# Node stage after the distance layer of a graph network: attention terms as 16 more columns of the table product, one row buffer for both tables, two PSUM banks per step

## The reference

```python
# layer 0, after its edges have been summed into agg
out = agg @ w2.T + b2
out = ssp(out) @ w3.T + b3
x = x + out                                   # written as x1
# layer 1, per node
h = jnp.maximum(_layernorm(x, axis=-1), 0.0)
hh = (h @ W0.T).reshape(n, 8, 32)             # written as tab1
a_s = jnp.sum(hh * att_src, axis=-1)          # 8 per node
a_d = jnp.sum(hh * att_dst, axis=-1)          # 8 per node
```

## Time and profile before

| what | us |
|---|---|
| median of 3 runs (lowest, highest) | 5398.98 (5395.08, 5399.30) |
| the profiled execution's own time | 5395.97 |
| span of that profile | 5394.1 |
| stage n1: its first transfer is issued at | 1451.24 |
| stage n1: its last table tile is written to SBUF by | 1667.7 |
| first transfer of the next stage is issued at | 1676.9 |
| PE busy in 1505 to 1621 (116 us) | 111.67 |
| DVE busy in the same stretch | 76.71 |
| ACT busy in the same stretch | 31.23 |

### The profile page before, as it was taken

One profiled execution on the slowest core, in us unless ns is written; L12 is line 12 of the kernel. 1 busy time (PEld: TensorE's weight loads), 2 busy tenths in 40 slices (PEclk: granted clock), 3 DMA queues, 4 the chain that ended last, 5 costly groups with the idle time before them and its releaser, 6 DMA issues. The chain is left out here.

```text
span 5394.1 us, 106431 instructions
## 1 busy us (share of the span) xinstructions
PE 4401.4 (82%) x24965; PEld 3546.0 (66%) x24965; DVE 3865.9 (72%) x8445; ACT 1994.5 (37%) x3783; POOL 3395.0 (63%) x3492
## 2 busy tenths in 40 slices
PE   5999999999895888888885655555556899999793
PEld 4888888888675888888884555555555566666431
DVE  5999999999764887888788544444446677877673
ACT  3666666666424655655554300000003000000370
POOL 2677777777414777777640477777773777777473
PEclk8999999999997988999897777777787999999796
DMA  6333333333234555555535333333335111111243
GB/s 199 115 105 103 103 104 103 104 105 102 79 117 110 135 127 126 129 125 129 123 84 158 111 110 109 109 109 109 107 104 162 39 40 40 38 35 29 61 114 109
DMA packets 452024, 555.48 MB, mean 103 GB/s; under 512 B 213168, under 2 KB 322148, under 8 KB 451552
## 3 DMA queue, kind: packets, MB, share of 16 engines
q0 software_dynamic: 154128, 374.88, 25.6%
q1 hardware_dynamic: 290585, 172.07, 11.8%
q10 hardware_dynamic: 6840, 3.36, 0.3%
HBM read 497.40 MB, written 59.40 MB: 103 GB/s over the span
## 5 line engine op out<-in xcount | busy, mean ns | idle before, releaser
L507 POOL DMA_INDIRECT l_rows<-tmp_tab,l_idx x832 | 882.2, 1060 | 376.2 <-issue 252.2
L1170 POOL DMA_INDIRECT l_rows<-tmp_tab,src_sb x832 | 791.8, 952 | 321.8 <-issue 236.1
L1890 POOL DMA_INDIRECT l_rows<-tmp_tab,src_sb x812 | 767.7, 945 | 253.0 <-issue 236.5
L1976 PE MATMUL l_psa<-l_sel,l_rows 128*128 128x128 f32 x3248 | 571.2, 348 | 413.2 <-issue 222.6
L1976 PEld LDWEIGHTS l_psa<-l_sel,l_rows 128*128 128x128 f32 x3248 | 529.9, 255 | 454.5 <-issue 256.2
L2128 POOL DMA_INDIRECT l_rows<-tmp_tab,src_sb x695 | 656.5, 945 | 235.5 <-issue 201.3
L805 PE MATMUL l_psw<-l_fw,l_ssp 128*128 128x256 f32 x3328 | 763.2, 382 | 0.0
L1916 DVE TENSOR_TENSOR acc<-acc,l_psa 128x256 f32 x832 | 350.9, 422 | 536.8 <-PE l_psa L1976 445.1
L805 PEld LDWEIGHTS l_psw<-l_fw,l_ssp 128*128 128x128 f32 x3328 | 616.0, 190 | 154.1 <-issue 77.3
L2239 PE MATMUL l_found<-l_tabs,l_hot 128*128 128x384 f32 (+1 forms) x1872 | 651.7, 502 | 0.0
L1490 PE MATMUL l_psa<-l_sel,l_rows 128*128 128x128 f32 x3328 | 597.7, 308 | 57.2 <-DVE acc L1390 55.4
(11 more groups left out here) (355 smaller groups left out, 7747.8 us busy)
## 6 DMA issues: line engine op xcount, KB each, us to landing
l_rows<-tmp_tab,src_sb POOLq DMA_INDIRECT x2339
l_edge<-in_edge_t SPq DMA_DIRECT2D x104, 256.0 KB
l_own<-tmp_tab SPq DMA_DIRECT2D x1280, 1.0 KB
l_own<-tmp_tab ACTq DMA_DIRECT2D x1280, 1.0 KB
l_own<-tmp_tab ACTq DMA_DIRECT2D x1280, 0.2 KB
l_own<-tmp_tab SPq DMA_DIRECT2D x1280, 0.2 KB
tmp_x<-n_X SPq DMA_DIRECT2D x39, 512.0 KB
n_X<-in_x SPq DMA_DIRECT2D x26, 512.0 KB
```

The source lines that it names most:

```text
L507: nc.gpsimd.indirect_dma_start(out=rows[r][:, t, :], out_offset=None, in_=table[:, :], in_offset=bass.IndirectOffsetOnAxis(ap=idx[q][:, j: ...
L1170: nc.gpsimd.indirect_dma_start(out=rows[r][:, j, :], out_offset=None, in_=dram["tab1"][:, :], in_offset=bass.IndirectOffsetOnAxis(ap=sh["s ...
L1890: nc.gpsimd.indirect_dma_start(out=rows[g % ROWS][:, t, :], out_offset=None, in_=table[:, :], in_offset=bass.IndirectOffsetOnAxis(ap=sh["s ...
L1976: last = nc.tensor.matmul(by_tile(g)[0:n, t, k * P:(k + 1) * P], left[:, f:f + n], sel[b][:, t, :], start=True, stop=True)
```

## The change

`nodes_schnet` is rewritten. What it computes and stores is the same.

- `watt` is copied behind the 256 columns of `gat_w_t` into one matrix `wt` of 272 columns, so a table tile is two products of 272 columns, and the 128x16 products go. The bias row `gb` gets 16 zeros.
- The 272 columns of a tile are written to `O` by one DVE addition; ACT's two copies and the buffer `A` go. Both stores on POOL read `O` (columns 0 to 263 for `tab1`, 256 to 271 for `att_tab`).
- PSUM: `psZ` for `hidden`, `psY` for `output`, `psT` for the transposes, `psW` for the tables, two banks each and one copy of each. `hidden` waits for the softplus of the chunk ahead, `output` for the addition of the one ahead. The tables go tile by tile through the two banks of `psW`: tile t waits until tile t-2 has been added into `O`.
- Four chunks behind instead of three: PE's step is `hidden`, `output`, `turn` (the transposes, two behind), `tables` (three behind). DVE splits the table work: tiles 0 and 1 between softplus and the residual, tiles 2 and 3 in the next step between cap and softplus.
- Three row buffers `X` instead of two.
- Loads: `w2` and `b2` first, with a semaphore of their own, so `hidden` of chunk 0 waits for these alone. The 16 attention vectors are issued by POOL. The product that makes `watt` stands after `hidden` of chunk 0 on PE.
- No semaphore starts above zero, so `begin` adds nothing and runs no second barrier.

```diff
-        O = pair_of(ph, "O", [P, CT, D + HEADS])
-        A = pair_of(ph, "A", [P, CT, 2 * HEADS])
-        psO = psum_pair(ph, "psO")
+        X = [ph.sb(f"X{r}", [P, CT, D]) for r in range(RX)]
+        norm, O = pair_of(ph, "norm", [P, CT, D]), pair_of(ph, "O", [P, CT, WT])
+        psZ, psY, psT, psW = (ph.ps(n, 1024) for n in ("psZ", "psY", "psT", "psW"))
...
+                sp.dma_start(w2[:, :, :], by_half(dram["w2_t"])).then_inc(w2_in, 16)
+                sp.dma_start(b2[:, :], dram["b2"][:, :]).then_inc(w2_in, 16)
+                sp.dma_start(w3[:, :, :], by_half(dram["w3_t"])).then_inc(w3_in, 16)
+                sp.dma_start(b3[:, :], on_all(dram["b3"], D)).then_inc(w3_in, 16)
+                load(0)
+                sp.dma_start(wt[:, :, 0:D], by_half(dram["gat_w_t"])).then_inc(wt_in, 16)
...
+            def _(pool):
+                pool.wait_ge(att_zero, 1)
...
+                        pool.dma_start(att[p:p + HID, h * HID // P, j * HEADS + h:j * HEADS + h + 1],
...
+                for n in range(CHUNKS):
+                    pool.wait_ge(o_done, (n + 1) * CT)
+                    pool.dma_start(node_rows(dram["tab1"], n), O[n % 2][:, :, 0:D + HEADS]).then_inc(o_stored[n % 2], 16)
+                    pool.dma_start(node_rows(dram["att_tab"], n), O[n % 2][:, :, D:WT]).then_inc(o_stored[n % 2], 16)
...
-                        nc.scalar.activation(O[c.p][:, :, D:D + HEADS], att_ps[:, :, 0:HEADS], ACT.Copy)
...
-                        nc.scalar.activation(A[c.p][:, :, :], att_ps, ACT.Copy).then_inc(a_done, 1)
...
+                def step(new, out, mid, old, last):
+                    if mid is not None:
+                        deviations(mid)
+                    if new is not None:
+                        exponential(new)
+                        logarithm(new)
+                    if mid is not None:
+                        relu(mid)
...
+                def table(n, tiles):
+                    if tiles[0] == 0:
+                        after(dve, o_stored[n % 2], 32 * (n // 2))
+                    for t in tiles:
+                        dve.wait_ge(tile_done, n * CT + t + 1)
+                        nc.vector.tensor_tensor(O[n % 2][:, t, :], psW[:, t % 2 * 512:t % 2 * 512 + WT], gb[:, :],
+                                                ALU.add).then_inc(o_done, 1)
...
+                def step(new, out, mid, old, last):
+                    if mid is not None:
+                        normalize(mid)
+                    if new is not None:
+                        cap(new)
+                    if last is not None:
+                        table(last, (2, 3))
+                    if new is not None:
+                        softplus(new)
+                    if new == 0:
+                        weights()
+                    if old is not None:
+                        if old == 0:
+                            dve.wait_ge(wt_in, 48)
+                        table(old, (0, 1))
+                    if out is not None:
+                        residual(out)
...
+                def hidden(n):
+                    after(pe, ssp_done, n)
...
+                def output(n):
+                    pe.wait_ge(ssp_done, n + 1)
+                    after(pe, y_added, n)
+                    project(nc, psY, ssp[n % 2], w3).then_inc(y_done, 1)
...
+                def tables(n):
+                    pe.wait_ge(hT_done, n + 1)
                     for t in range(CT):
+                        after(pe, o_done, n * CT + t - 1)
                         for k in range(KH):
-                            nc.tensor.matmul(nm.psT[c.p][:, t * 2 * HEADS:(t + 1) * 2 * HEADS],
-                                             nm.hT[c.p][:, k, t * P:(t + 1) * P], watt[:, k, :],
-                                             start=(k == 0), stop=(k == KH - 1))
-                    project(nc, psO[c.p], nm.hT[c.p], wg).then_inc(mm_done, 1)
+                            last = nc.tensor.matmul(psW[:, t % 2 * 512:t % 2 * 512 + WT], hT[n % 2][:, k, t * P:(t + 1) * P],
+                                                    wt[:, k, :], start=(k == 0), stop=(k == KH - 1))
+                        last.then_inc(tile_done, 1)
...
+                    if new is not None:
+                        hidden(new)
+                    if new == 0:
+                        weights()
+                    if out is not None:
+                        output(out)
+                    if mid is not None:
+                        turn(mid)
+                    if old is not None:
+                        tables(old)
```

More of the change, by code:

```diff
@@ L841, in nodes_schnet @@
 def nodes_schnet(nc, dram, sh, acc):
+    W2 = 2 * HEADS
+    WT = D + W2
+    RX = 3
     with Phase(nc, "n1") as ph:
[L844 to L851, removed]
@@ L947, in _, with deviations, exponential @@
-                staggered(act, step, 3)
+                def deviations(n):
+                    act.wait_ge(mv_done, n + 1)
+                    nc.scalar.activation(std[n % 2][:, :], mv[n % 2][:, :, 1], ACT.Ln, bias=sh["eps"][:, 0:1]).then_inc(log_done, 1)
+                    act.wait_ge(log_done, n + 1)
+                    after(act, norm_done, n - 1)
+                    nc.scalar.activation(rstd[n % 2][:, :], std[n % 2][:, :], ACT.Exp, scale=-0.5).then_inc(std_done, 1)
+                def exponential(n):
+                    act.wait_ge(z_done, n + 1)
+                    after(act, y_done, n - 1)
+                    for k in range(KH):
+                        last = nc.scalar.activation(ssp[n % 2][:, k, :], psZ[:, k * CN:(k + 1) * CN], ACT.Exp, bias=b2[:, k:k + 1])
+                    last.then_inc(exp_done, 1)
@@ new lines, in logarithm, with relu @@
+                def logarithm(n):
+                    act.wait_ge(cap_done, n + 1)
+                    nc.scalar.activation(ssp[n % 2][:, :, :], ssp[n % 2][:, :, :], ACT.Ln, bias=1.0).then_inc(ln_done, 1)
+                def relu(n):
+                    act.wait_ge(xT_done, n + 1)
+                    after(act, tile_done, (n - 1) * CT)
+                    flat = hT[n % 2][:, :, :].rearrange("p k n -> p (k n)")
+                    for lo, hi in BANKS:
+                        last = nc.scalar.activation(flat[:, lo:hi], psT[:, lo:hi], ACT.Relu)
+                    last.then_inc(hT_done, 1)
@@ L959, in _, with normalize @@
-                dve.wait_ge(bias_done, 1)
-                def softplus(c):
-                    dve.wait_ge(exp_done, c.n + 1)
-                    flat = ssp[c.p][:, :, :].rearrange("p k n -> p (k n)")
+                def normalize(n):
+                    dve.wait_ge(std_done, n + 1)
+                    after(dve, xT_done, n - 1)
+                    for t in range(CT):
+                        last = nc.vector.tensor_scalar(norm[n % 2][:, t, :], X[n % RX][:, t, :], mv[n % 2][:, t, 0:1],
+                                                       rstd[n % 2][:, t:t + 1], ALU.subtract, ALU.mult)
+                    last.then_inc(norm_done, 1)
@@ L997, in step @@
[L997 to L1007 removed]
+                    dve.wait_ge(y_added, n + 1)
+                    nc.vector.tensor_tensor(x[:, :, :], x[:, :, :], b3[:, :].unsqueeze(1).to_broadcast([P, CT, D]),
+                                            ALU.add).then_inc(x_done, 1)
@@ new lines, in tables, with step @@
+                        last.then_inc(tile_done, 1)
+                def step(new, out, mid, old, last):
+                    if new is not None:
[8 more added lines that the diff above has]
+                        tables(old)
+                pe.wait_ge(w2_in, 32)
@@ L1065, in edges_gat @@
+                unrolled(step)
 def edges_gat(nc, dram, sh, acc):
```

245 lines of the change are left out of this document (102 added, 143 removed).

## The result

| kernel | median us (lowest, highest), runs | ratio to the kernel before, 95% interval |
|---|---|---|
| before | 5397.58 (5395.08, 5399.30), 4 | |
| changed | 5363.27 (5357.32, 5366.58), 4 | 0.9936 [0.9918, 0.9953] |

The change takes off 34.3 us, 0.64%, well over the 0.2% that the prediction took as the least that can be told from no change; forecast were 5365 us and faster. The sum is right to 2 us, but its terms are not: stage n1 gave 6 us more than forecast, and the program behind it gave part of that back.

What follows compares the result with a forecast made beforehand. PE was taken to bound the middle of stage n1. Terms -21.9 - 13.8 - 1.6 + 2 + 1 = -34.3 took the profiled 5395.97 us to 5361.7; with 3.0 for the median, 5365 us, range 5352 to 5382.

Steps and rivals of the forecast that it cites:

- term 1: Middle of stage n1, hidden of chunk 3 to hidden of chunk 12: 103.3 us against 125.18 before, -21.9.
- the wait of 0.66: Middle step before the change: PE waits 0.66 us for the newest chunk's softplus; goes if the chains beside PE are shorter.
- Its circles: Middle: three dependency chains beside PE, 8.3, 10.7 (DVE) and 10.1 us, all under PE's 11.38 a step.
- term 2: Start of stage n1, up to hidden of chunk 3: it starts at 1483.9 against 1497.67, -13.8.
- the small ones: Additions to the sum: +2 for a clock dip from idle patches of the start, +1 for hand-overs beyond the chains.
- the chain's 8.3: Hidden to the next hidden over psZ: 3.64 us to the exponential, 4.66 through cap, logarithm and softplus to PE.
- term 3: End of stage n1, from hidden of chunk 12: -1.6 us, between -9.5 and +0.3.
- H: Start of hidden of chunk 12, from which the end is timed; last addition forecast to end at 35.4 at full clock.
- Vectors late: Rival at the start: POOL at 1.25 us per transfer, hidden 1 starts 9.3 us later: 5374 us; chance 0.12.
- DVE paces the middle: Rival: additions of 0.65 and slower hand-overs lift DVE's circle to 12.1 us, total 5371; chance 0.10.
- the wide product saves nothing: Rival: the 16 columns cost their 1.78 us inside the 272-column product too, +20, total 5385; chance 0.03.
- both clock rivals: Middle's clock at 0.78: +29, 5394 us, no change, chance 0.04; at 0.67: +51, 5416 us, slower, chance 0.03.

Runs made afterwards that it cites:

- the split: Changed kernel with the 16 attention columns as products of their own again, still one addition of 272 columns: 5378.84 us, ratio 0.9964.
- the two kernels made for them: Changed kernel with added 128x1024 DVE additions ahead of each residual (one 5370.31 us, two 5388.03), and changed kernel with the 16 columns as separate products (5378.84 us).
- the extra additions: Changed kernel with one or two more 128x1024 additions on DVE ahead of each residual: 5370.31 and 5388.03 us, one run each.

## Why the prediction held, and where it did not

**The middle, term 1: -21.9 forecast, -21.7 measured.** `hidden` 3 to `hidden` 12 took 103.45 us (1485.85 to 1589.30) against a forecast of 103.3: steps of 11.71, seven of 11.43 and one of 11.73. The reasoning held in each part: PE alone bounds it (busy 103.41 of 103.50 us), the wide addition took 0.44 (0.45 was chosen), and the 16-column products were paid by the product, which the split shows by itself (1.57 of the 2.29 us a step). The other 0.72 is what the forecast put on the wait of 0.66 and the gap of 0.11; that fits, but no run undoes it. Its circles were on the safe side (DVE 10.13 against 10.7).

**The start, term 2: -13.8, with +2 of the small ones, forecast; -11.8 measured** (1485.85 against 1497.67). The total is right by errors that cancel. The step that failed is "the attention vectors on POOL cost nothing". They were issued as fast as assumed, 0.49 to 0.56 us each, but the last was there 6.9 us after its issue instead of 2.8, at 1463.9 instead of 1462, and `hidden` 1 stood behind it, 2.5 us after its softplus. By the Trainium skill, "DMA: Bandwidth & Descriptors", section "Issuing engine by pattern", simple loads belong on Sync; with the vectors there they came 1.5 us earlier, but X1 and X2 moved behind them in the same run, so the trace doesn't decide it. The same page's 2.0 us fixed time of a GpSimd transfer (section "Anatomy of one DMA") is less than the 4.7 to 6.9 us of the last of sixteen here, but those ran beside full DMA engines, so no run here measures it. What the forecast left out is that traffic: its 2.8 us were read from one small load on SP, without asking what else moves at the time. `hidden` 1 then ran mostly at the lower clock, and `hidden` 2 came 10.84 us behind it, 2.5 more than the chain's 8.3, which the small +2 covered. On the other side, the stage began 1.3 us earlier than forecast, because the phase ahead ended 1.0 earlier in that execution, `hidden` 0 waited only 3.35 us for its weights, not 3.7, and it took 5.77 us (1452.39 to 1458.16), not 6.86. The last two, 0.35 and 1.09, and the earlier start are 2.7 us, and they hid the 2.5 of the vectors: `hidden` 1 started at 1465.58, forecast 1465.8. Of the barrier that the change saves, 1.2 us show: from the last addition of the phase ahead to the first transfer 0.86, against 2.06 in both profiles of the kernel before.

**The end, term 3: -1.6 forecast, -7.1 measured.** From `hidden` 12 to the end of the last addition 37.73 us, against 44.87 before. The chain was right: turn 11 at H + 16.59 (forecast 16.7), turn 12 at H + 26.34 (26.6). The size that was off is the clock's. The last 8.2 us of work were put at 0.57, +6.2, and another +1.7 for one more dip. Measured, the last stretch took 11.39 us at 0.77 against 8.8 forecast for full clock, +2.6, and nothing else dipped. A mean of one window of the kernel before was taken as if the clock were low for the whole of whatever follows an idle stretch. The two profiles of the kernel before differ in just this place (44.87 and 42.86 us from `hidden` 12 to the end), so such a price should have been a range; against the second, term 3 is -5.1.

**Behind the stage: 0 forecast.** The sentence "what follows the last table tile is the same in both kernels" was wrong by 0.9 us: from the end of the last addition to the next stage's first transfer 10.09 in place of 9.17. In the one profile with the vectors on SP it was 8.75, so the place of these sixteen transfers seems to be paid there too. And from there to the end of the program the two profiles of the changed kernel have 3727.7 and 3726.7 us, those of the kernel before 3717.2 and 3723.2, which is mostly the spread of one stage (1160.7 to 1170.1). All twelve profiles of the new order lie between 3719.8 and 3729.3, so the second one of the kernel before lies among them. By medians some 4 to 5.5 us of the 39.8 are missing, and 2 to 3.5 where its second profile is taken (next stage at 1674.90). What takes them stays open: with two profiles of the kernel before, luck and a small lasting effect of the change can't be told apart.

What parts of the change are worth, each by undoing it alone: the joined products 17 us, the weight products behind `hidden` 0 10 to 11, the third row buffer 0. The order in which the table additions are split over two steps keeps PE the bound; without it the last addition begins 186.11 us after the first transfer, 8.6 to 9.6 later. These are not shares of the 40.7, since they overlap, and neither the change from paired to separate PSUM buffers nor the fourth chunk behind nor the dropped barrier was undone by itself.

**The rivals.** "Vectors late" happened in kind, at 2.5 us and not 9: POOL kept its 0.5 us pace, and the delay lay between the last issue and its landing. "DVE paces the middle" and "the wide product saves nothing" are refuted by the two kernels made for them. From `hidden` 4 to `hidden` 12 PEclk was 1.00 in all twelve profiles of the new order (only with the extra additions it was 0.87 and 0.89 between `hidden` 3 and 4), so both clock rivals fall; the Trainium skill's rule on PSUM cycling ("TensorE: Matmul & The Clock Gate", section "A second HAM failure mode: psum-queue depth-cycling") does not bite in this ring of two banks, where the hand-over hides under the next tile's products and PE was busy 103.41 of 103.50 us.

## What to carry to other kernels

Price narrow products by the product, not by the column: in float32, 16 columns ran at 0.37 us for two of them per tile and at 0.06 as a wider edge of a product that is there anyway. Small loads that something waits for want a place ahead of the big ones that nothing waits for yet, and the products that need them a place in PE's order behind work that is ready; the second was shown by itself (2.3 to 3.3 us), the first only together with a change of engine. At the end of a stage look for the order on DVE that leads to the last PE work: a moved residual won 3.5 us in one kernel and 5.0 in another, 1.0 and 2.5 of it by the earlier start of the last transposes and 2.5 by the clock behind them.

## What the runs showed of the hardware that was not expected

- Sixteen small POOL loads issued 0.49 us apart were complete only 4.7 to 6.9 us after the last was issued, with the DMA share at 0.98 or more (1458 to 1461); the same loads on SP (issued 0.46 apart), with the share at 0.05, were complete 1.9 us after. Which of the two differences matters is open.
- The same wait of 2.40 us on PE near the end of the stage was followed by four products at PEclk 0.55 in one kernel and at 1.00 in another that has the same order there: 3.59 and 2.10 us.
- From the end of the last DVE addition to the next stage's first transfer all eleven other profiles of the changed order had 10.1 us, and the one with the vectors on SP 8.75, though those loads were over 165 us earlier. Why is open.
- The same stage, with the same 7384 matmul records, took 1160.7 to 1170.1 us in fourteen executions, and a phase in front of n1 ended up to 5 us apart in kernels that do not differ there. One profile of each side is too little to place a difference of 5 us.
